# A list of its own for the second and third hop of a graph propagation, and the first hop's sums moved out in pieces

## The chip, the cores and the metric
One core of one Trainium2 chip runs the program once. The metric is the device time of that execution in microseconds (us). The engines are TensorE (PE, with its weight loads PEld), VectorE (DVE), ScalarE (ACT), GpSimd (POOL) and SyncE (SP, which here only issues DMAs). DVE-, ACT-, POOL- or PEq in the profile is an engine's sequencer.

## The reference
A graph has 100,000 nodes with 32 features (`x`) and 25,000 edges `src -> dst`, sorted by `dst`. Four layers follow each other, each with a layer norm behind it: a tensor-product convolution with a small radial network, a three-hop propagation, an edge network with a maximum per node, and an attention layer. The change is in the second:

```
deg = segment_sum(ones, dst);  norm = deg[src]**-.5 * deg[dst]**-.5   (0 where deg is 0)
x = weight;  acc = weight
for _ in range(3):
    x = segment_sum(norm[:, None] * x[src], dst)
    acc = acc + x
return acc / 4
```

Only nodes that some edge points to have a value after the first hop, so an edge carries something in the second hop only if its source has an incoming edge, in the third only if that edge's source has one too.

## The kernel before
**Layout.** Edges lie in tiles of 128 partitions by T = 196 columns, in order of `dst`; the sums of a run of equal `dst` are scans along the columns, one VectorE instruction for each of 32 features (L1378), with a "seam" (L1331) that carries a run over from one partition to the next through two small TensorE transposes. Values are fetched by row with indirect DMAs, one column of 128 rows per instruction, issued by POOL. Nodes that no edge points to need no edges; their layers collapse to a chain of norms and products, done in "node chunks" (13 of 128 x 60 rows and a tail of 40 x 4 rows): TensorE turns and multiplies (L1136), ScalarE copies and squares (L867), VectorE reduces and scales (L1731). `node_chunks` (L426) runs them; `NODE_PAIRS` (L423) says which pairs of chunks run in which of four windows: two pairs, two pairs, two pairs, and the last chunk with the tail.

**Start.** VectorE zeroes A_dst, SP stores it as zeros to `edge_sums` and tables 1 and 2 (L472), 3,136 KB each, then loads the 20 weights (L489); VectorE waits for those (L1463) before it folds them and starts the histogram of `dst`. POOL waits for the zeros (L658) before it gathers into A_dst.

**Short list.** `make_short` (L1557, VectorE, within the first layer) picks in each partition the edges whose source has an incoming edge, and moves them to the front in order with MAX8 and MATCH_REPLACE (`take_top`, L1606) on three keys: the table index, the flags and degree, and the output column. The longest partition gives n. FEWEST = 60 columns are always moved, FEW = 64 are computed; if n is larger, branches handle up to T columns.

**Propagation.** `short_columns` (L676, POOL) moves the list's columns and then raises `short_in`. Per hop k = 0, 1, 2 (L699) POOL waits for the table and for a free buffer, then gathers 60 columns. VectorE does its node window, waits for `short_in`, and runs `propagate` (L1767): scan, clear the buffer for the next gather, seam, multiplication by dinv_short, add to A_tmp, multiplication again for the table, which SP stores (L546 to L552). After the third hop POOL scatters the accumulated sums A_tmp to `edge_sums`, again 60 columns (L707). SP loads `edge_sums` back into A_msg by seven chunks, then the edge attributes into A_tmp (L554 to L560). VectorE meanwhile computes statistics of A_src (L1797 to L1812), then `add_layer1` (L1813) adds the sums to A_dst, `norm` normalises chunk by chunk, and SP stores each chunk to table 3 (L561). POOL's 196 gathers of the next layer wait for that table (L712); it then sends a quad of four columns at a time and waits for the quad before the last to land.

ScalarE and TensorE follow the same windows in order (L885, L1162); a seam stands behind each.

Of the kernel before, what the change touches and what calls it, by code (L numbers as in the profile page):

```python
# [31 lines left out]
FEWEST = 60  # L32
TOP = -(-T // 8) * 8
# [22 lines left out]
def parts_until(k):  # L56
    return sum(TABLE_PARTS[:k + 1])
# [19 lines left out]
def gnn_kernel(nc, x, src, dst, r_feat, rel, edge_attr, edge_weight, w1, b1, w2, b2,  # L77
# [12 lines left out]
    with ExitStack() as ctx:  # L90
# [13 lines left out]
        tables = [dram(f"table_{k}", (E_PAD, FEAT if k else FEAT + 1)) for k in range(5)]  # L104
# [66 lines left out]
        n_short = sb("n_short", [1, 1], i32)  # L171
        row_base = sb("row_base", [P, 1])
# [7 lines left out]
        diag = sb("diag", [P, P])  # L180
        seam_state = sb("seam_state", [32, P])
# [49 lines left out]
        few_done, more_done, rest_done = sem("few_done"), sem("more_done"), sem("rest_done")  # L231
        short_in = sem("short_in")
# [55 lines left out]
        short_row_i = dst_f[:].bitcast(i32)  # L288

# [133 lines left out]
        NODE_PAIRS = [(0, 2, False), (2, 4, False), (4, 6, False), (6, D_CHUNKS // 2, True)]  # L423
# [30 lines left out]
        def _(sp):  # L454
# [17 lines left out]
            for zeroed in (edge_sums, tables[1], tables[2]):  # L472
                sp.dma_start(zeroed.rearrange(main3, t=T), A_dst[:]).then_inc(zeros_stored, 16)
# [72 lines left out]
            for k in (1, 2):  # L546
                sp.wait_ge(table_ready, parts_until(k))
                table = tables[k].rearrange(main3, t=T)
                with sp.If(n > FEW):
                    sp.dma_start(table, A_sum[:]).then_inc(table_stored, 16)  # L550
                with sp.Else():
                    sp.dma_start(table[:, 0:FEW, :], A_sum[:, 0:FEW, :]).then_inc(table_stored, 16)  # L552
                node_chunks(sp, load_nodes, ahead[k], ahead[k + 1], k == 2)
# [35 lines left out]
        def _(pool):  # L589
# [68 lines left out]
            pool.wait_ge(zeros_stored, 48)  # L658
# [15 lines left out]
            turns = [0]  # L674

            def short_columns(move, keep=None):  # L676
                turns[0] += 1
                for t in range(FEWEST):
                    if keep and keep(t):
                        pool.wait_ge(n_out, keep(t))  # L680
                    move(t).then_inc(few_done, 16)
                with pool.If(n > FEWEST):
                    for t in range(FEWEST, FEW):
                        move(t).then_inc(more_done, 16)
                    pool.wait_ge(more_done, 16 * (FEW - FEWEST) * turns[0])
                with pool.If(n > FEW):
                    for t in range(FEW, T):
                        move(t).then_inc(rest_done, 16)
                    pool.wait_ge(rest_done, 16 * (T - FEW) * turns[0])
                pool.wait_ge(few_done, 16 * FEWEST * turns[0])  # L690
# [8 lines left out]
            for k in range(3):  # L699

                pool.wait_ge(table_stored, 16 * parts_until(k))
                pool.wait_ge(gather_ok, k + 2)
                to, idx = (A_msg, idx_next) if k else (msg_wide, idx_short)
                short_columns(take_short(lambda t: to[:, t, :], tables[k], idx),
                              None if k else lambda t: max(t - 24, 0) // 15)
            pool.wait_ge(acc_ready, 1)
            short_columns(lambda t: pool.indirect_dma_start(  # L707
                out=edge_sums, out_offset=bass.IndirectOffsetOnAxis(ap=out_short[:, t:t + 1], axis=0),
                in_=A_tmp[:, t, :], in_offset=None, bounds_check=edge_limit, oob_is_err=False))
# [29 lines left out]
        def _(act):  # L739
# [144 lines left out]

            for window in NODE_PAIRS:  # L885
                nodes(*window)
# [146 lines left out]
        def _(pe):  # L1033
# [229 lines left out]
        def _(v):  # L1263
# [293 lines left out]
            def make_short():  # L1557
# [76 lines left out]
                step(ts(dinv_short[:], keys[:, 0, :].bitcast(i32), 1.0, ALU.max))  # L1634

# [5 lines left out]
                step(ts(keys[:, 0, :].bitcast(i32), top_i[:, 2, own], 255, ALU.bitwise_and))  # L1641
                step(ts(run, keys[:, 0, :].bitcast(i32), row_base[:], ALU.add, float(-SKIP), ALU.add))
# [124 lines left out]
            def propagate(k, width):  # L1767

                a_sum, a_msg, acc = A_sum[:, 0:width, :], A_msg[:, 0:width, :], A_tmp[:, 0:width, :]
                by = bcast(dinv_short[:, 0:width], FEAT)  # L1770
                if k == 0:
                    v.tensor_copy(idx_next[:, 0:width], msg_wide[:, 0:width, FEAT].bitcast(i32))
                step(scan(a_sum, a_msg if k else msg_wide[:, 0:width, 0:FEAT], same_short, ALU.mult, ALU.add, 0.0))
                if k < 2:
                    v.memset(a_msg, 0.0).then_inc(gather_ok, 1)
                seam(a_sum, FEAT, 0, 1, in_first_short, ALU.mult, ALU.add, 0.0)
                step(tt(a_sum, a_sum, by, ALU.mult))
                ins = tt(acc, acc, a_sum, ALU.add) if k else v.tensor_copy(acc, a_sum)
                if k < 2:
                    step(ins)  # L1780
                    done(tt(a_sum, a_sum, by, ALU.mult), table_ready, parts_until(k + 1))
                else:
# [327 lines left out]
```

## Time and profile before

| what | us |
|---|---|
| median of 3 runs | 2012.31 (2007.58 to 2029.45) |
| profiled execution | 2009.45 |
| its span, first to last instruction | 2007.7 |
| POOL busy | 1419.7 |
| VectorE busy | 1323.3 |
| TensorE busy | 1026.2 |

Idle time of an engine is shown in brackets with what ended it. "Chain" is the sequence of work that ended last, followed back from the end. An indirect DMA's time on POOL is the making of its descriptors, not the transfer; the chain shows a transfer as DMA from issue to landing. "issue" is time in which an engine waited for nothing that the profile shows.

### The profile page before, as it was taken

To read this page: it belongs to the slowest core of one execution; us is meant where nothing else is said; L and a number is where in the kernel's file an instruction comes from. 1 tells how busy PE (TensorE), PEld (TensorE's weight loads), DVE (VectorE), ACT (ScalarE), POOL (GpSimd) and SP (SyncE) were. 2 spreads that over 40 slices of the span, in tenths; PEclk is the share of its full clock that TensorE was granted. 3 is DMA by queue.
4 is the path that set the end of the run, shared out by engine and by line. 5 is a ranking of instruction groups with operands and counts; after the bars stand their busy time and mean duration, and the time that the engine had idled before them with its cause. 6 is when DMAs were issued, how large, how long until landed. Compare 5 with 4: busy or idle time off the path is not lost.

```text
span 2007.7 us, 15353 instructions
## 1 busy us (share of the span) xinstructions
PE 1026.2 (51%) x3969; PEld 700.3 (35%) x3969; DVE 1323.3 (66%) x3061; ACT 468.6 (23%) x989; POOL 1419.7 (71%) x1304
## 2 busy tenths in 40 slices
PE   0989737872770353407020069888458767613100
PEld 0334414441430353406020035545257767613000
DVE  6989949998999774727364653435667788875000
ACT  0954301110110341405121122222112233311000
POOL 7887777775778484855757277777277777777776
PEclk9985555555555676859565555555555555655555
DMA  7008611110002231303100600000001110100000
GB/s 261 11 11 286 216 12 13 13 13 9 12 13 67 89 112 64 119 21 121 42 27 8 193 4 4 22 13 13 29 22 27 27 24 25 27 11 11 11 11 10
DMA packets 65924, 101.54 MB, mean 51 GB/s; under 512 B 35491, under 2 KB 54693, under 8 KB 65060
## 3 DMA queue, kind: packets, MB, share of 16 engines
q1 hardware_dynamic: 23074, 74.87, 10.7%
q0 software_dynamic: 40832, 12.83, 4.6%
q10 hardware_dynamic: 1922, 12.80, 1.6%
q8 instruction: 31, 0.51, 0.1%
q14 instruction: 65, 0.53, 0.1%
HBM read 55.72 MB, written 52.06 MB: 54 GB/s over the span
## 4 chain that ended last, share of the span: by engine, by line
POOL 41%; DVE 30%; issue 16%; PE 8%; DMA 3%; SPq 2%; ACT 0%; POOLq 0%; DVEq 0%; PEld 0%; PEldq 0%; ACTq 0%
POOL A_src L626 17%; POOL A_msg L694 11%; POOL out L733 10%; DVE work L1279 9%; DVE work L1290 6%; PE bank L1078 4%; POOL edge_sums L707 4%; DVE A_sum L1378 2%; DVE A_dst L1279 2%; DVE stat L1290 1%; DVE A_msg L1279 1%; SPq L489 1%; PE bank L1035 1%; DVE A_tmp L1279 1%; DVE A_sum L1279 1%
## 5 line engine op out<-in xcount | busy, mean ns | idle before, releaser
L626 POOL DMA_INDIRECT A_src<-table,pos_i x392 | 424.4, 1083 | 193.1 <-issue 122.8
L626 POOL DMA_INDIRECT A_dst<-in_x,dst_i x196 | 225.3, 1149 | 75.4 <-issue 58.3
L1118 PE MATMUL bank<-w2fold,work 65*128 65x384 f32 x392 | 262.2, 849 | 3.6 <-ACT work L811 3.1
L1035 PE MATMUL bank<-ident,work 128*65 128x128 f32 (+2 forms) x592 | 153.0, 390 | 197.0 <-DVE work L1279 106.4
L733 POOL DMA_INDIRECT out<-A_dst,out_i x196 | 201.5, 1028 | 62.4 <-issue 62.4
L1290 DVE TENSOR_REDUCE work<-work 128x96 f32<-128x768 f32 (+5 forms) x245 | 210.4, 907 | 49.6 <-ACT work L840 41.4
L694 POOL DMA_INDIRECT A_msg<-table,idx_next x120 | 147.7, 1231 | 89.0 <-DMA table<-A_sum 50.4
L1035 PE MATMUL bank<-ident,end_col 128*32 128x128 f32 (+2 forms) x16 | 6.0, 377 | 397.0 <-DVE end_col L1335 392.9
L1035 PEld LDWEIGHTS bank<-ident,work 128*65 128x65 f32 (+2 forms) x592 | 98.5, 194 | 260.2 <-DVE work L1279 142.1
L626 POOL DMA_INDIRECT A_src<-x_pos,A_tmp x140 | 145.2, 1037 | 46.6 <-issue 46.3
L1279 DVE TENSOR_TENSOR work<-bank,work 128x256 f32<-128x256 f32 (+1 forms) x392 | 164.0, 477 | 4.6 <-PE bank L1118 4.6
L1118 PEld LDWEIGHTS bank<-w2fold,work 65*128 65x128 f32 x392 | 124.0, 331 | 96.8 <-issue 89.8
L1157 PE MATMUL bank<-nodes_w,small 128*128 128x128 f32 (+1 forms) x784 | 119.6, 313 | 45.2 <-ACT small L830 45.0
L1035 PEld LDWEIGHTS bank<-ident,end_col 128*32 128x32 f32 (+2 forms) x16 | 1.5, 92 | 400.1 <-DVE end_col L1335 395.5
L1287 DVE SCALAR_TENSOR_TENSOR A_sum<-A_sum,same_pen,bank 128x32 f32<-128x32 f32 x195 | 48.2, 247 | 134.0 <-PE bank L1191 128.8
L811 ACT ACTIVATE work<-bank,b1col 65x256 f32<-65x256 f32 x98 | 45.9, 470 | 378.2 <-PE bank L1035 378.0
L1157 PEld LDWEIGHTS bank<-nodes_w,small 128*128 128x128 f32 (+1 forms) x784 | 110.5, 224 | 53.6 <-ACT small L830 53.6
L1191 PEld LDWEIGHTS bank<-mw,work 65*128 65x128 f32 x392 | 87.3, 328 | 77.2 <-issue 77.2
L694 POOL DMA_INDIRECT A_msg<-table,nxt_i x60 | 73.6, 1227 | 42.3 <-DMA table<-A_tmp 24.3
L707 POOL DMA_INDIRECT edge_sums<-A_tmp,out_short x60 | 73.4, 1223 | 37.3 <-issue 20.6
L1184 PE MATMUL bank<-work,mw 96*64 96x512 f32 x98 | 96.5, 1087 | 0.0
L1191 PE MATMUL bank<-mw,work 65*128 65x32 f32 x392 | 93.7, 404 | 0.0
(298 smaller groups left out, 2231.5 us busy)
## 6 DMA issues: line engine op xcount, KB each, us to landing
work<-in_x SPq DMA_DIRECT2D x26, 960.0 KB
x_pos<-A_sum SPq DMA_DIRECT2D x13, 990.0 KB, 5.3
out<-work ACTq DMA_DIRECT2D x13, 960.0 KB, 3.8
table<-A_dst SPq DMA_DIRECT2D x2, 3136.0 KB, 22.7
table<-A_dst SPq DMA_DIRECT2D x14, 448.0 KB, 4.0
A_src<-table,pos_i POOLq DMA_INDIRECT x392, 2.3
A_tmp<-in_edge_attr_2x SPq DMA_DIRECT2D x49, 112.0 KB
table<-A_tmp SPq DMA_DIRECT2D x7, 462.0 KB, 2.5
```

Source lines behind the costliest of these rows:

```text
L626: pool.indirect_dma_start(out=column(t), out_offset=None, in_=of, in_offset=bass.IndirectOffsetOnAxis(ap=idx[:, t:t + 1], axis=0), bounds_ ...
L694: return lambda t: pool.indirect_dma_start(out=column(t), out_offset=None, in_=of, in_offset=bass.IndirectOffsetOnAxis(ap=idx[:, t:t + 1], ...
L707: short_columns(lambda t: pool.indirect_dma_start(out=edge_sums, out_offset=bass.IndirectOffsetOnAxis(ap=out_short[:, t:t + 1], axis=0), i ...
L733: pool.indirect_dma_start(out=out, out_offset=bass.IndirectOffsetOnAxis(ap=out_i[:, t:t + 1], axis=0), in_=A_dst[:, t, :], in_offset=None, ...
L1035: return nc.tensor.transpose(out_ap, in_ap, ident[0:n, 0:n])
L1078: last = nc.tensor.matmul(banks[6 + h][:, 0:half], lo_hot[:, 2 * slot + j, :], hi_hot[:, 2 * slot + j, h * half:(h + 1) * half], start=Fal ...
L1118: last = nc.tensor.matmul(banks[2 + 2 * slot + j][:, 0:PATHS], hidT[:, slot, j * P:(j + 1) * P], w2fold[:], start=True, stop=True)
L1157: last = nc.tensor.matmul(banks[2 + 2 * w + s][0:parts, k * P:(k + 1) * P], n_xT[:, s, k * parts:(k + 1) * parts], nodes_w[:, w * P:(w + 1 ...
L1184: nc.tensor.matmul(banks[2 + slot][0:HID0, :], mw1[:], catT[:, slot, :], start=True, stop=True).then_inc(e_h, 1)
L1191: last = nc.tensor.matmul(banks[4 + slot][:, j * FEAT:(j + 1) * FEAT], hidT2[:, slot, j * P:(j + 1) * P], mw2[:], start=True, stop=True)
L1279: return v.tensor_tensor(out=o, in0=a, in1=b, op=op)
L1290: return v.tensor_reduce(out=o, in_=a, axis=AX, op=op)
```

## The change
A second list is built in VectorE after the first hop: of the short list's edges those whose source's own sum has a source in the list, at most FEWEST2 = 22 columns moved and FEW2 = 24 computed. The first hop fetches with each value the row's place in the short list; table 1 gets a 33rd column with the place in the second list. The first hop's sums no longer join the accumulator: they are scattered from A_sum to `edge_sums`, 12 columns after the first hop, 12 behind the second hop's gathers, 36 behind the third's. The second and third hop's sums go to a buffer `edge_sums2`, 22 columns. Both are loaded back and added one after the other. `edge_sums2` and the wider table 1 must be zeroed too. Node windows become three pairs, one, one, and the rest (chunks 10 to 12 and tail). The edge attributes are loaded after the exchange of table 3. If a partition's second list is longer than 24, `use_short_list` goes on with all T columns.

```diff
+FEW2 = 24
+FEWEST2 = 22
+FIRST_OUT = [12, 24]
...
-        NODE_PAIRS = [(0, 2, False), (2, 4, False), (4, 6, False), (6, D_CHUNKS // 2, True)]
+        NODE_PAIRS = [(0, 3, False), (3, 4, False), (4, 5, False), (5, D_CHUNKS // 2, True)]
...
-            for zeroed in (edge_sums, tables[1], tables[2]):
+            wide = tables[1].rearrange("(p t) f -> p (t f)", t=T)
+            sp.dma_start(wide[:, 0:T * FEAT], flat(A_dst[:])).then_inc(zeros_stored, 16)
+            sp.dma_start(wide[:, T * FEAT:], A_dst[:, 0:T // FEAT + 1, :].rearrange("p t f -> p (t f)")[:, 0:T]).then_inc(zeros_stored, 16)
+            for zeroed in (edge_sums, edge_sums2, tables[2]):
...
+            sp.wait_ge(first_hop_out, 16 * FEWEST)
             sp.wait_ge(short_in, 4)
+            sp.wait_ge(acc_ready, 1)
             for c in range(CHUNKS):
                 sp.dma_start(chunk(A_msg, c), chunk(edge_sums.rearrange(main3, t=T), c)).then_inc(sums_in[c], 16)
+            sp.wait_ge(hop_done, 16 * FEWEST2 * 3)
+            sp.wait_ge(short_in, 5)
+            for c in range(CHUNKS):
+                sp.dma_start(chunk(A_tmp, c), chunk(edge_sums2.rearrange(main3, t=T), c)).then_inc(sums2_in[c], 16)
+            exchange(3, A_dst)
             for a, b in PIECES:
                 sp.dma_start(A_tmp[a:b], edge_attr[a * T:b * T, :].rearrange(main3, t=T)).then_inc(ea_in, 16)
...
-            exchange(3, A_dst)
             exchange(4, A_dst, LAST_ORDER)
...
+            first_out = put_short(edge_sums, out_short, lambda t: A_sum[:, t, :])
+            pool.wait_ge(first_hop_ready, 1)
+            short_columns(first_out, first_hop_out, range(FIRST_OUT[0]))
+            pool.wait_ge(table_stored, 16 * parts_until(1))
+            pool.wait_ge(gather_ok, 3)
+            n2 = pool.value_load(n_short2[0:1, 0:1], min_val=0, max_val=T)
+            second_columns(take_short(lambda t: msg_wide[:, t, :], tables[1], idx2))
+            short_columns(first_out, first_hop_out, range(*FIRST_OUT))
+            pool.wait_ge(table_stored, 16 * parts_until(2))
+            pool.wait_ge(gather_ok, 4)
+            second_columns(take_short(lambda t: A_msg[:, t, :], tables[2], idx2))
+            short_columns(first_out, first_hop_out, range(FIRST_OUT[1], FEWEST))
             pool.wait_ge(acc_ready, 1)
+            second_columns(put_short(edge_sums2, out2, lambda t: A_tmp[:, t, :]))
...
+            nodes(*NODE_PAIRS[0])
+            next_root(1.0)
+            for window in NODE_PAIRS[1:]:
                 nodes(*window)
...
+                if first == 0:
+                    pe.wait_ge(count_ready, 2)
+                    turn(banks[6][0:1, 0:P], end_col[:, 0:1], P).then_inc(count_turned, 1)
...
+            def first_hop(width):
+
+                a_sum, by = A_sum[:, 0:width, :], bcast(dinv_short[:, 0:width], FEAT)
+                v.tensor_copy(idx_next[:], msg_wide[:, :, FEAT].bitcast(i32))
+                step(scan(a_sum, msg_wide[:, 0:width, 0:FEAT], same_short, ALU.mult, ALU.add, 0.0))
                 seam(a_sum, FEAT, 0, 1, in_first_short, ALU.mult, ALU.add, 0.0)
+                done(tt(a_sum, a_sum, by, ALU.mult), first_hop_ready, 1)
+                tt(tmp_wide[:, 0:width, 0:FEAT], a_sum, by, ALU.mult)
+
+            def second_list():
+
+                step(v.tensor_copy(idx_f, idx_next[:, 0:FEW]))
+                step(ts(kept2, idx_f, SKIP / 2, ALU.is_lt))
+                step(tt(kept2, kept2, ends_row, ALU.max))
+                step(v.memset(kept2[:, 0:1], 1.0))
+                done(total(end_col[:, 0:1], kept2), count_ready, 2)
...
+                for r in range(FEW2 // 8):
+                    at = slice(8 * r, 8 * r + 8)
+                    for k in range(3):
+                        ins = v.max(out=top2[:, k, at], in_=keys2[:, k, :])
                     step(ins)
+                    for k in range(3):
+                        ins = v.match_replace(out=keys2[:, k, :], in_to_replace=top2[:, k, at], in_values=keys2[:, k, :],
+                                              imm_value=0.0)
+                    step(ins)
...
+            def use_second_list():
+
+                few = slice(0, FEW2)
+                v.tensor_copy(dinv2[:, few], std[:, few])
+                v.tensor_copy(idx2[:, few], idx2_new)
+                step(v.memset(msg_wide[:, few, :], 0.0))
+                v.memset(msg_wide[:, few, FEAT].bitcast(i32), SKIP).then_inc(gather_ok, 1)
+                done(v.tensor_copy(stat[:, few], dinv2[:, few]), table_ready, parts_until(1))
+
+            def second_hop(width, to_table):
+
+                acc, by = A_tmp[:, 0:width, :], bcast(dinv2[:, 0:width], FEAT)
+                v.tensor_copy(idx2[:, 0:width], msg_wide[:, 0:width, FEAT].bitcast(i32))
+                step(scan(acc, msg_wide[:, 0:width, 0:FEAT], same2, ALU.mult, ALU.add, 0.0))
+                if width == FEW2:
+                    v.memset(A_msg[:, 0:width, :], 0.0).then_inc(gather_ok, 1)
+                seam(acc, FEAT, 0, 1, in_first2, ALU.mult, ALU.add, 0.0)
+                step(tt(acc, acc, by, ALU.mult))
+                done(tt(to_table, acc, by, ALU.mult), table_ready, parts_until(2))
...
+            v.wait_ge(count_turned, 2)
+            step(total(end_col[0:1, 1:2], banks[6][0:1, 0:P], ALU.max))
+            root(v.tensor_copy(n_short2[:], end_col[0:1, 1:2]))
+            n2 = v.value_load(n_short2[0:1, 0:1], min_val=0, max_val=T)
...
             node_chunks(v, nodes, *NODE_PAIRS[3])
 
+
+            for c in range(CHUNKS):
+                v.wait_ge(sums_in[c], 16)
+                last = stt(chunk(A_dst, c), chunk(A_msg, c), 0.25, chunk(A_dst, c), ALU.mult, ALU.add)
+            step(last)
...
             def add_layer1(c):
-                v.wait_ge(sums_in[c], 16)
-                return stt(chunk(A_dst, c), chunk(A_msg, c), 0.25, chunk(A_dst, c), ALU.mult, ALU.add)
+                v.wait_ge(sums2_in[c], 16)
+                return stt(chunk(A_dst, c), chunk(A_tmp, c), 0.25, chunk(A_dst, c), ALU.mult, ALU.add)
```

`make_short` gets six more small operations that keep, for 64 columns, what the second list needs. The third hop does what the second does without the memset and the table, and adds its sums to the second's.

## Rows read from the trace of the kernel before

**Rows 1.** The page of the profile: busy times, and chain by line
```profile
PE 1026.2 (51%) x3969; PEld 700.3 (35%) x3969; DVE 1323.3 (66%) x3061; ACT 468.6 (23%) x989; POOL 1419.7 (71%) x1304
...
POOL A_src L626 17%; POOL A_msg L694 11%; POOL out L733 10%; DVE work L1279 9%; DVE work L1290 6%; PE bank L1078 4%; POOL edge_sums L707 4%; DVE A_sum L1378 2%; DVE A_dst L1279 2%; DVE stat L1290 1%; DVE A_msg L1279 1%; SPq L489 1%; PE bank L1035 1%; DVE A_tmp L1279 1%; DVE A_sum L1279 1%
```

**Rows 2.** The page's costliest groups: moves of a list's columns
```profile
L694 POOL DMA_INDIRECT A_msg<-table,idx_next x120 | 147.7, 1231 | 89.0 <-DMA table<-A_sum 50.4
...
L707 POOL DMA_INDIRECT edge_sums<-A_tmp,out_short x60 | 73.4, 1223 | 37.3 <-issue 20.6
```

**Rows 3.** DVE's timeline, 694 to 797 us: start, duration, instruction, idle before
```profile
694.22 2.15 DVE L1290 TENSOR_REDUCE work<-work 128x60 f32<-128x1920 f32 x1 [10.88 <-ACT work L840]
...
743.56 2.15 DVE L1290 TENSOR_REDUCE work<-work 128x60 f32<-128x1920 f32 x1 [1.38 <-ACT work L840]
...
754.44 2.16 DVE L1279 TENSOR_TENSOR work<-work 128x1920 f32<-128x1920 f32 x1
773.57 0.22 DVE L1772 COPY idx_next<-A_msg 128x64 int32<-128x64 int32 x1 [16.98 <-POOLq L691]
...
780.15 1.76 DVE L1775 MEMSET A_msg<- 128x2048 f32 x1 [0.49 <-DVE A_sum L1378]
...
785.38 2.29 DVE L1279 TENSOR_TENSOR A_sum<-A_sum,small 128x2048 f32<-128x2048 f32 x1 [0.24 <-DVE A_sum L1279]
...
796.59 2.15 DVE L1290 TENSOR_REDUCE work<-work 128x60 f32<-128x1920 f32 x1 [5.33 <-ACT work L840]
```

**Rows 4.** POOL's timeline, 796 to 883 us, same columns
```profile
796.47 0.99 POOL L694 DMA_INDIRECT A_msg<-table,idx_next  x1 [24.68 <-DMA table<-A_sum]
797.76 1.00 POOL L694 DMA_INDIRECT A_msg<-table,idx_next  x1 [0.30 <-issue]
...
882.41 1.00 POOL L694 DMA_INDIRECT A_msg<-table,idx_next  x1 [2.95 <-issue]
```

**Rows 5.** Window of one move: length, busy PE, PEld, DVE, ACT, POOL, clock, DMA share, GB/s
```profile
796.00:892.50 96.50, 30.12 (x219) 27.89 (x219) 48.13 (x36) 28.39 (x62) 74.12 (x60) 0.71 0.23 81
```

**Rows 6.** The chain in order of time, 770 to 1124 us: start, duration, what
```profile
770.79 2.12 DMA A_msg<-table,nxt_i
...
791.45 4.75 DMA table<-A_sum
...
1120.32 3.42 DMA A_msg<-edge_sums
```

**Rows 7.** DVE's timeline, 1047 to 1124 us
```profile
1047.38 6.68 DVE L1290 TENSOR_REDUCE stat<-A_src 128x196 f32<-128x6272 f32 x1
...
1054.39 6.71 DVE L1279 TENSOR_TENSOR A_src<-A_src,stat 128x6272 f32<-128x6272 f32 x1
...
1078.02 6.69 DVE L1279 TENSOR_TENSOR A_src<-A_src,small 128x6272 f32<-128x6272 f32 x1
1123.84 2.11 DVE L1287 SCALAR_TENSOR_TENSOR A_dst<-A_msg,A_dst 128x896 f32<-128x896 f32 x2 [39.12 <-DMA A_msg<-edge_sums]
```

**Rows 8.** DVE's timeline in the making of the first list, 479 to 490 us
```profile
479.31 0.89 DVE L1609 MAX8 A_sum<-A_sum 128x8 f32<-128x196 f32 x3
...
486.44 0.47 DVE L1623 CAST A_sum<-A_sum 128x600 int32<-128x600 f32 x1 [3.06 <-DVEq L1622]
...
489.54 0.26 DVE L1283 TENSOR_SCALAR small<-A_sum 128x196 f32<-128x196 int32 x1
```

**Rows 9.** POOL's timeline beside a long DVE multiplication, and the gather's start
```profile
1055.67 6.29 POOL L707 DMA_INDIRECT edge_sums<-A_tmp,out_short  x1 [0.31 <-issue]
...
1152.87 2.31 POOL L626 DMA_INDIRECT A_src<-table,pos_i  x1 [33.73 <-DMA table<-A_dst]
```

**Rows 10.** SP's timeline, the stores of zeros
```profile
8.52 0.90 SPq L473 DMA_DIRECT2D table<-A_dst  x2
```

**Rows 11.** The chain in order of time, before the histogram
```profile
34.40 6.80 DMA gw<-in_L_gnn_W
```

**Rows 12.** Window in the stores of zeros, columns as in rows 5
```profile
20.00:25.00 5.00, 0.70 (x3) 0.26 (x2) 2.11 (x8) 0.00 (x0) 3.78 (x5) 1.00 1.07 430
```

More of the change, by code:

```diff
@@ L171, in gnn_kernel @@
         n_short = sb("n_short", [1, 1], i32)
+        n_short2 = sb("n_short2", [1, 1], i32)
+        end_column, edges_in, ends_row = (r3[:, FEW * k:FEW * (k + 1)] for k in range(3))
+        same2, in_first2, dinv2, idx2, out2 = dst_f, r3, dinv, idx_next, nxt_i
         row_base = sb("row_base", [P, 1])
@@ L180, in gnn_kernel @@
         diag = sb("diag", [P, P])
+        slot_key, slot_ones = diag[:, 0:FEW], diag[:, FEW:2 * FEW]
         seam_state = sb("seam_state", [32, P])
@@ L673, in _, with short_columns @@
             n = pool.value_load(n_short[0:1, 0:1], min_val=0, max_val=T)
[L674 to L678, printed above, removed]
+            turns = {"short": 0, "second": 0}
+            def short_columns(move, done, columns, keep=None):
+                for t in columns:
                     if keep and keep(t):
                         pool.wait_ge(n_out, keep(t))
-                    move(t).then_inc(few_done, 16)
+                    move(t).then_inc(done, 16)
+                if columns.stop < FEWEST:
+                    return
+                turns["short"] += 1
                 with pool.If(n > FEWEST):
@@ L688, in short_columns, with second_columns @@
                         move(t).then_inc(rest_done, 16)
-                    pool.wait_ge(rest_done, 16 * (T - FEW) * turns[0])
-                pool.wait_ge(few_done, 16 * FEWEST * turns[0])
+                    pool.wait_ge(rest_done, 16 * (T - FEW) * turns["short"])
+                pool.sem_inc(short_in, 1)
+            def second_columns(move):
+                turns["second"] += 1
+                for t in range(FEWEST2):
+                    move(t).then_inc(hop_done, 16)
+                with pool.If(n2 > FEWEST2):
+                    for t in range(FEWEST2, FEW2):
+                        move(t).then_inc(hop_more, 16)
+                    pool.wait_ge(hop_more, 16 * (FEW2 - FEWEST2) * turns["second"])
+                with pool.If(n2 > FEW2):
+                    for t in range(FEW2, T):
+                        move(t).then_inc(hop_rest, 16)
+                    pool.wait_ge(hop_rest, 16 * (T - FEW2) * turns["second"])
                 pool.sem_inc(short_in, 1)
@@ new lines, in third_hop @@
+            def third_hop(width):
+                acc, msg, by = A_tmp[:, 0:width, :], A_msg[:, 0:width, :], bcast(dinv2[:, 0:width], FEAT)
+                step(scan(msg, msg, same2, ALU.mult, ALU.add, 0.0))
+                seam(msg, FEAT, 0, 1, in_first2, ALU.mult, ALU.add, 0.0)
+                step(tt(msg, msg, by, ALU.mult))
+                done(tt(acc, acc, msg, ALU.add), acc_ready, 1)
+            node_chunks(v, nodes, *NODE_PAIRS[0])
+            v.wait_ge(few_done, 16 * FEWEST)
+            v.wait_ge(short_in, 1)
@@ new lines, in _ @@
+            before_it = dict(count)
+            seq_after = count["seq"] + 100
+            with v.If(n > FEW):
+                first_hop(T)
+                step(v.memset(stat[:], 1.0))
+                done(v.memset(end_col[:, 0:1], float(T)), count_ready, 2)
+                v.sem_inc(dve_seq, seq_after - count["seq"])
+            count.update(before_it)
+            with v.Else():
+                first_hop(FEW)
+                second_list()
+                v.sem_inc(dve_seq, seq_after - count["seq"])
@@ L1786, in _ @@
+            with v.If(n2 > FEW2):
+                use_short_list()
+                v.sem_inc(dve_seq, seq_after - count["seq"])
+            count.update(before_it)
+            with v.Else():
+                use_second_list()
+                v.sem_inc(dve_seq, seq_after - count["seq"])
+            count["seq"] = seq_after
+            for k, hop in ((1, lambda width: second_hop(width, A_msg[:] if width == T else A_msg[:, FEW:FEW + FEW2, :])),
+                           (2, third_hop)):
                 node_chunks(v, nodes, *NODE_PAIRS[k])
+                v.wait_ge(hop_done, 16 * FEWEST2 * k)
```

136 lines of the change are left out of this document (97 added, 39 removed).

## The prediction

> **What bounds the kernel now.** I read the page first [rows 1]: POOL is the busiest engine (71%) and carries the chain of work that ended last; the lines this change touches, L694 and L707, hold 11% and 4% of it. In the costliest groups [rows 2] these are four moves of 60 columns, at 1.23 us of descriptor work per column. Then the timeline: in the first node window VectorE handles a chunk every (743.56 - 694.22) / 3 = 16.4 us, is done at 754.44 + 2.16 = 756.6 and idles 16.98 us until POOL's last column has landed [rows 3]. A bare column costs 1.00 + 0.30 = 1.30 us, 60 cost 78 us [rows 4], yet the move fills a window of 96.5 us: it has one gap of 2.95 us [rows 4], a landing, and columns that are stretched while VectorE multiplies, 74.1 us of busy time instead of 60 [rows 5], or 3.5 us for each of the four node chunks. After a move come the hop's sums on VectorE and a store of 4.75 us; only then does POOL start again [rows 3, 4, 6], 24.68 us after it stopped. After the last move VectorE has been idle for 39.12 us [rows 7]. So from 680 to 1124 us POOL's columns and the gaps between hops set the time, and VectorE's work hides beside them. What the change is worth is read there: at 1124 us everything behind follows as before.
>
> **Part by part.** All on the clock of the profiled execution, shifts of the start left for later.
>
> *First window, one chunk pair longer.* Two chunks more: 756.6 + 2 x 16.4 = 789.4. The first hop, which started at 773.57, now waits for VectorE: 16 us lost.
>
> *First hop.* From the copy of the next indices to the first multiplication it took 785.38 - 773.57 = 11.8 us, of which the memset and its wait (2.0) go; with the multiplication (2.3) the sums are ready at 789.4 + 9.8 + 2.3 = 801.5 [rows 3]. POOL then issues 12 scatters (12 x 1.30 = 15.6, about 2 more beside the second multiplication) and is done at 819, before it is needed.
>
> *Second list.* New on the path: a multiplication (2.3); some 39 small operations and 3 rounds of MAX8 and replacing, at 64 or 24 columns; count, turn and a root with a reciprocal over 196 columns; register loads, two branches; a memset of 24 columns. At 196 columns a small operation takes 0.26 us and three MAX8 0.89, and leaving a branch cost 3.06 us [rows 8]. Upper bound: 39 x 0.3 + 3 x 2.05 + 4 + 3 x 3.1 + 4 = 35 us; lower, at 0.15 us each and branches for nothing: 17 us. I take 24: the operations are a third as wide but have a fixed part, and the branch behind the seam cost 0.24 us [rows 3]. Table ready at 825.5, stored (wider rows, same count, 4.75 plus issue [rows 6]) at 830.7; POOL loads its register and gathers from 831.7. ScalarE's root stands ahead of the next window, so that window's first chunk is ready only some 12 us after 820 (before, it came 796.59 - 785.38 = 11.2 us after the seam [rows 3]).
>
> *Hop 2.* 22 columns x 1.30 = 28.6, plus 6 for one and a half node chunks beside it: landed at 867.4. VectorE's two chunks end at 833 + 16.4 + 13 = 862, in time (a last chunk takes 756.6 - 743.56 = 13). The sums: 11.8 us with a smaller memset, 10.7, and two multiplications of 24 columns at 0.9: 12.4, so 880.5. Its scans stay 32 instructions, and I claim nothing for their being narrower. The store of 384 KB takes about 3 us. POOL meanwhile issues 12 scatters: two skipped branches (3, by the gap of rows 4), 15.6 and 1.4 of stretching: 886.3. Here POOL is last by 3 us.
>
> *Hop 3.* 28.6 + 7.2: landed 923.4; VectorE's two chunks, ready 11.2 us after the seam at 879, end at 920. Sums without memset: 0.7 to start, 9.8 + 1.8, so 935.7, with the seam done at 933.9.
>
> *Last window.* Chunks 10 to 12 and the tail (the old last window was one chunk and tail): first reduction at 933.9 + 11.2 = 945.1, end 945.1 + 2 x 16.4 + 13 + 3 = 994 (3 is what I put for the tail of 40 partitions and 4 rows). POOL's 36 scatters run beside it: 923.4 + 3 + 46.8 + 9 = 982, landed and loaded back (3.42 [rows 6]) at 988, so hidden. VectorE then adds seven chunks (7 x 1.09) and does the statistics of A_src, which ran from 1047.38 to 1078.02 + 6.69 = 1084.7, 37.3 us [rows 7], hidden beside POOL before and exposed now: 994 + 7.6 + 37.3 = 1039.
>
> *Last scatter.* 22 columns from 982: 28.6 plus stretching by VectorE's two-input operations. One such operation on all of A_src (6.71 us) held one column for 6.29 us [rows 7, 9]. With 14 us of stretching, landing and load: about 1031. Hidden by 8 us.
>
> The norm began at 1123.84 [rows 7], now at 1039: **84.8 us gained**. The Trainium skill (SBUF — State Buffer, Who interferes with whom) infers that a two-input tensor operation does not stall descriptor generation; rows 7 and 9 show that it does here, and the row decides: I give the page's rule no chance of its own. By the page hop 2 and hop 3 would each lose their stretching, and the sum would be some 10 us lower.
>
> *Zeros.* SP issues two more large stores ahead of the weight loads, 3.3 MB more. Issue alone is 0.45 us each [rows 10], 0.9. VectorE waits for the last weight at 41.2 us, on the chain [rows 11]. The stores run at 430 GB/s with all DMA engines full [rows 12], so 3.3 MB are 7.7 us if the weights queue wholly behind them. I take 4, since the last weight's 6.80 us already hold some queueing, and keep 0.9 and 8. The Trainium skill (DMA: Bandwidth & Descriptors, Queues, rings and completion order) says that descriptors of one ring are consumed in order; that speaks for the upper end, and would put the sum 4 us higher.
>
> *First list.* Six more small operations on VectorE, on the chain: 6 x 0.2 = 1 us (0 to 2).
>
> *Edge attributes.* Their load, 3.1 MB, moves behind the exchange of table 3. The exchange loses that company (it took 1152.87 - 1123.84 = 29 us to the first gather [rows 7, 9]; 0 to 3 us gained), while the load, 7.5 to 12 us by 430 GB/s or a load's lower rate, meets the first gathers of the next stage. I take +0.5 in all, bounds -3 and +10. VectorE needs the attributes 25 us later, after the spread.
>
> Sum: -84.8 + 4 + 1 + 0.5 = -79.3. The profiled execution took 2009.45 us (span 2007.7), so 1930; the median shown is 2.9 above it: **1933 us**.
>
> **Rivals.**
> *POOL stays last.* For: its last scatter has 8 us of slack in a sum with 40 us of stretching and skipped branches, and the gap of 2.95 us may come at every one of six branches. Against: the VectorE side is a sum of measured pieces. If POOL needs 20 us more, 12 show: 1945.
> *The edge attributes collide.* POOL waits for quads to land, and the next stage goes at POOL's pace. If nothing lands for the load's 12 us: 1933 + 10 = 1943. Against: with the DMA engines full of zeros POOL issued gathers at its usual pace, 3.78 us busy in 5 [rows 12], though nothing made it wait for them to land.
> *The weights wait for all the zeros.* The stores fill the engines [rows 12] and the weights come behind them on the same queue: 7.7 us instead of 4, 1937. Against: the last weight landed some 8 us after the stores' time was up (9.6 MB by 430 GB/s from 8.5 us), so it does not simply come behind them. This is what the page's rule of ring order gives.
> *The zeros cost nothing and the list is cheap (17 us).* 1933 - 3 - 7 = 1923.
> *The other side: the second list does not fit.* If one partition keeps over 24 columns, both hops and the second scatter move 196 columns. Then 60 + 3 x 196 columns stand where 180 stood: 468 x 1.30 = 608 us more, 2620 us. It decides at 25. The trace cannot show it; counting the reference's edges by the rule of the diff gives at most 22 kept columns, 12.7 on average, so nearly excluded. It is also the way in which the change would not do what it says.
>
> **How the numbers follow.** Forecast case 0.50; weights wait for all zeros 0.10; POOL last 0.15; collision 0.10; cheap list and zeros 0.08; not fitting 0.01; the rest, 0.06, for a wait that I have not seen. The range goes from 1916 (all lower bounds: list -7, zeros -3, edge attributes -3, narrower scans -4) to 1958 (list +11 and a rival's 12). A measurement here tells about 1% from no change. Faster by over 1% needs under 1992, which all cases but the last two give: 0.95. Within 1%: 0.03. Slower: 0.02.
>
> **What would show it.** Right: POOL's gathers of the two hops at 22 columns in some 35 us each; first sums ready at 801.5 instead of 787.7, plus the start's shift; in hop 3's wake VectorE busy without a gap up to the norm; the norm at about 1039 plus 5. Wrong: VectorE idle before the norm (POOL still last); more than 30 us between the first hop's sums and its table; the histogram starting over 8 us later; POOL's gaps between the first quads. Gathers of 196 columns would break the forecast altogether.

## The result and the profile after

The changed kernel took 1928.20 us (median of 4 runs, 1922.72 to 1943.07) against 2009.94 us for the kernel before on the same chip: ratio 0.959, 95% interval 0.950 to 0.967. The profiled execution took 1925.58 us, its span is 1923.8 us. Forecast were 1933 us, 1930 on the profile's own clock. Later, on another chip, the ratio was 0.959 again (0.955 to 0.962), and on one more 1.013; that one has a place of its own below.

The page, busy times and two of the costliest groups, as in [rows 1, 2]:

```profile
PE 1020.9 (53%) x3970; PEld 696.9 (36%) x3970; DVE 1330.1 (69%) x3146; ACT 466.6 (24%) x990; POOL 1366.5 (71%) x1250
...
L747 POOL DMA_INDIRECT edge_sums<-A_sum,out_short x60 | 74.0, 1234 | 51.0 <-DVE A_sum L1345 33.0
...
L741 POOL DMA_INDIRECT A_msg<-table,nxt_i x60 | 73.4, 1224 | 40.0 <-DMA table<-A_tmp 22.1
```

A column costs what it did. POOL lost 53 us of busy time, 54 columns; that the time fell by 84 says that gaps went too. Where the end of the stage now comes from, DVE's timeline shows; its last row answers to the last of [rows 7]:

```profile
799.52 0.34 DVE L1842 COPY idx_next<-A_msg 128x196 int32<-128x196 int32 x1 [0.83 <-DVE work L1345]
...
841.13 2.15 DVE L1356 TENSOR_REDUCE work<-work 128x60 f32<-128x1920 f32 x1 [9.25 <-ACT work L901]
...
874.84 0.41 DVE L1929 COPY idx_next<-A_msg 128x24 int32<-128x24 int32 x1 [4.40 <-DMA A_msg<-table,idx_next]
...
928.72 3.66 DVE L1444 TENSOR_TENSOR_SCAN A_msg<-dst_f,A_msg 128x24 f32<-128x24 f32 x32 [6.49 <-DMA A_msg<-table,idx_next]
...
1003.76 6.69 DVE L1356 TENSOR_REDUCE stat<-A_src 128x196 f32<-128x6272 f32 x1
...
1010.77 6.69 DVE L1345 TENSOR_TENSOR A_src<-A_src,stat 128x6272 f32<-128x6272 f32 x1
...
1034.39 6.69 DVE L1345 TENSOR_TENSOR A_src<-A_src,small 128x6272 f32<-128x6272 f32 x1
1041.12 2.09 DVE L1353 SCALAR_TENSOR_TENSOR A_dst<-A_tmp,A_dst 128x896 f32<-128x896 f32 x2
```

The norm's first row has no bracket: before, VectorE had stood still for 39.12 us there [rows 7], now it comes straight from the statistics. It is VectorE that sets this end; its only waits for POOL's data behind the first window are 4.40 and 6.49 us, in front of the second and third hop. Its other long waits there are of 9 us each, when a window's first chunk comes through TensorE and ScalarE, and one of 5.57 us for ScalarE's squares within the statistics. Inside hops 2 and 3 POOL's gathers still land last, by those 4.40 and 6.49 us; from the third hop's sums on, VectorE has no wait for POOL's data.

The time splits into three parts, by three rows that both kernels have: POOL's first column of the first hop (680.16 before, 687.82 now), the norm (1123.84 and 1041.12), the end.

| stretch | predicted | measured |
|---|---|---|
| start to POOL's first column | +5 | +7.7 |
| from there to the norm | -84.8 | -90.4 |
| from the norm to the end | +0.5 | -1.2 |
| sum | -79.3 | -83.9 |

How far such a split can be trusted, a second profile of the changed kernel shows, on the chip of run 12:

```profile
1037.63 2.09 DVE L1353 SCALAR_TENSOR_TENSOR A_dst<-A_tmp,A_dst 128x896 f32<-128x896 f32 x2
```

Its first column came at 686.95 us, the norm 3.5 us earlier than here, and from the norm to the end it took 891.5 us, not 882.7. So 3 or 4 us at the norm, and more behind it, lie within what one kernel shows from one profile and chip to the next.

The start, DVE's timeline and then SP's in the stores of zeros:

```profile
49.68 0.82 DVE L1349 TENSOR_SCALAR w2fold<-A_tmp 65x64 f32<-65x64 f32 x6 [8.95 <-DMA gw<-in_L_gnn_W]
```

```profile
31.47 8.14 SPq L508 DMA_DIRECT2D gb<-in_L_gnn_b  x1
39.65 3.81 SPq L508 DMA_DIRECT2D gw<-in_L_gnn_W  x4
```

VectorE is ready at 40.7 us and waits 8.95 us for the last four weights, which SP came to only at 39.65 us: the issue before them took 8.14 us instead of the 1.1 to 1.3 of its neighbours.

### The profile page after: what moved, and what is told of

Its sections match the earlier page's. It is cut to its first block, busy times and chain, and to the rows that moved or that the text cites. A ratio compares the mean times of both kernels' runs of the same rounds, so it can differ in the third digit from the quotient of the medians.

```text
span 1923.8 us, 15361 instructions
## 1 busy us (share of the span) xinstructions
PE 1020.9 (53%) x3970; PEld 696.9 (36%) x3970; DVE 1330.1 (69%) x3146; ACT 466.6 (24%) x990; POOL 1366.5 (71%) x1250
## 4 chain that ended last, share of the span: by engine, by line
POOL 28%; issue 10%; DVE 9%; PE 5%; DMA 3%; ACT 1%; POOLq 0%; DVEq 0%; ACTq 0%; SPq 0%
POOL A_src L656 15%; POOL out L794 10%; POOL A_msg L741 3%; DMA A_src<-table,pos_i 2%; DVE work L1345 2%; PE bank L1257 1%; PE bank L1250 1%; DVE stat L1356 1%; PE bank L1098 1%; DVE A_dst L1345 1%; DVE A_dst L1353 1%; DVE A_src L1345 1%; PE bank L1220 1%; DVE A_sum L2156 1%; POOL edge_sums L747 0%
## 5 line engine op out<-in xcount | busy, mean ns | idle before, releaser
L656 POOL DMA_INDIRECT A_dst<-in_x,dst_i x196 | 230.3, 1175 | 76.2 <-issue 58.5
L1098 PEld LDWEIGHTS bank<-ident,work 128*65 128x65 f32 (+2 forms) x592 | 95.7, 190 | 267.5 <-DVE work L1345 142.8
L747 POOL DMA_INDIRECT edge_sums<-A_sum,out_short x60 | 74.0, 1234 | 51.0 <-DVE A_sum L1345 33.0
L1098 PE MATMUL bank<-ident,A_tmp 128*65 128x128 f32 (+1 forms) x203 | 50.4, 398 | 72.6 <-DVE A_tmp L2104 66.4
```

Of the source, the lines that this page charges most:

```text
L656: pool.indirect_dma_start(out=column(t), out_offset=None, in_=of, in_offset=bass.IndirectOffsetOnAxis(ap=idx[:, t:t + 1], axis=0), bounds_ ...
L747: return lambda t: pool.indirect_dma_start(out=of, out_offset=bass.IndirectOffsetOnAxis(ap=idx[:, t:t + 1], axis=0), in_=column(t), in_off ...
L1098: return nc.tensor.transpose(out_ap, in_ap, ident[0:n, 0:n])
```

## Experiments

All edits are to the changed kernel. Times of single profiled runs are named as such. The runs were made on several chips: the kernel before took 2003.11 us (7 runs) where runs 1 to 4 were made and 2009.00 us (7 runs) at runs 5 to 7, so times across them are compared as ratios to it.

**1. The weights ahead of all zeros.** SP's block of stores moves behind the loop of weight loads:

```diff
-            for zeroed in (edge_sums, edge_sums2, tables[2]): ...
             for to, of in (... weights ...):
                 sp.dma_start(to, of).then_inc(loaded_w, 16)
+            for zeroed in (edge_sums, edge_sums2, tables[2]): ...
```

> SP loads the 20 weights ahead of the five stores of zeros. Theory (the weights stood behind the zeros in SP's queue, and nothing else was late at the start): VectorE's wait of 8.95 us at 49.68 us goes wholly, so it folds the weights from about 40.7 us and the rest follows; time 1925.6 - 9 = 1917 us. The zeros land some 3 us later, which nobody sees, since POOL first needs them much later. Rival (the DMA engines' load as a whole delays the start, or something else is as late): the fold starts no earlier than about 45 us, 1921 to 1926 us.

Measured: VectorE folds the weights at 40.76 us with no wait, 8.9 us earlier. The norm starts at 1029.51 us, 11.6 us earlier, and the profiled run took 1912.68 us, 12.9 less than the changed kernel's, some of which may be the chip's. By median 1918.51 us, ratio 0.958 (0.953 to 0.964), which by itself tells nothing from 0.959: in times the gain is not resolved, in the trace the wait is gone and what follows is earlier. Of the 2.7 us that came on top by the norm, 1.7 are the first window's six chunks, which took 95.7 us instead of 97.4; run 12's profile of the changed kernel has 95.5, so this need not be the edit's.

**2. Only one store behind the weights.**

```diff
-            for zeroed in (edge_sums, edge_sums2, tables[2]):
+            for zeroed in (edge_sums, tables[2]):
...
+            sp.dma_start(edge_sums2.rearrange(main3, t=T), A_dst[:]).then_inc(zeros_stored, 16)
```

> Only the store of zeros to edge_sums2 (3.2 MB) goes behind the weights; the wider zeros of table 1 stay ahead. Theory (the delay is the time of the bytes ahead of the weights, 3.2 MB by some 415 GB/s = 7.7 us): VectorE's wait falls from 8.95 to between 0.6 and 1.5 us, time 1918 us. Rival (the wider table with its extra small store, or SP's waits for a free place in the queue, make the delay): over 3 us of the wait stay.

Measured, 1913.65 us in one run:

```profile
41.27 0.73 DVE L1350 TENSOR_SCALAR w2fold<-A_tmp 65x64 f32<-65x64 f32 x6 [0.55 <-DMA gw<-in_L_gnn_W]
```

The wait falls by 8.4 us with this one store of 3.2 MB, and the issue that took 8.14 us takes 1.33. The wider table 1 and its small extra store cost nothing that shows, so one more DMA ahead is not what delays. The delay fits the time of the bytes queued ahead: 3.2 MB at the 414 GB/s that moved between 10 and 40 us would be an estimated 7.7 us.

**3. The node windows of before.** `NODE_PAIRS` is two, two, two pairs, and the rest.

> The node windows of the kernel before (two, two, two pairs, the rest) with everything else of the change. Theory (VectorE's work with its gaps sets the time from the first hop to the norm, POOL is hidden): the first hop comes some 16 us earlier (VectorE idle that long in the first window), in exchange VectorE's waits of 4.4 and 6.5 us for POOL go, net 16 - 11 = 5 us more: norm at 1046, time 1931 us. Rival (POOL's columns set it, as before the change): the first hop's 16 us come through whole, 1910 us.

Measured: 1934.81 us, ratio 0.965 (0.959 to 0.972), norm at 1049.41. First window and second hop:

```profile
783.66 0.34 DVE L1842 COPY idx_next<-A_msg 128x196 int32<-128x196 int32 x1 [19.49 <-DMA A_msg<-table,nxt_i]
...
888.52 0.18 DVE L1929 COPY idx_next<-A_msg 128x24 int32<-128x24 int32 x1 [0.50 <-DVE work L1345]
```

The first hop comes 15.9 us earlier and the norm 8.3 later. The two waits for POOL are gone, as expected. The rival falls: POOL's columns no longer set this stretch. The 8.3 us are more than the 5 reckoned because the first window's wait is 19.49 us and not 16. Against 0.83 there that is 18.7 us more, while 3.9 and 5.7 us go in front of the second and third hop: 9.1 net. By the profiles the new windows are worth 8 us (12 by run 12's); the intervals of the medians overlap.

**4. A pair more in the third window**, (0, 3), (3, 4), (4, 6), the rest.

> Windows of three, one, two pairs, and the rest: the third window takes a pair from the last. Theory (VectorE bound): its wait of 6.49 us for the third hop's columns is filled with node work, the norm starts 6.5 us earlier, 1919 us; POOL's last scatter can start only at about 971 us instead of 938, but POOL has 36 others to send until 983 us. Rival (POOL or its landing decides the end): no gain or a loss, 1926 us or more.

Measured: 1925.81 us, ratio 0.960 (0.955 to 0.965); norm at 1037.66, 3.5 us earlier, 0.9 of them already there by the second hop. But run 12's profile of the changed kernel has it at 1037.63 too, so no gain is shown and the theory's 6.5 us did not come: the rival "no gain" stands. The node work does end 6.6 us earlier (3.1 against run 12), but then a new wait stands in VectorE's queue:

```profile
994.94 1.09 DVE L1353 SCALAR_TENSOR_TENSOR A_dst<-A_msg,A_dst 128x896 f32<-128x896 f32 x1 [1.79 <-DMA A_msg<-edge_sums]
996.82 2.20 DVE L1353 SCALAR_TENSOR_TENSOR A_dst<-A_msg,A_dst 128x896 f32<-128x896 f32 x2 [0.78 <-DMA A_msg<-edge_sums]
999.18 1.09 DVE L1353 SCALAR_TENSOR_TENSOR A_dst<-A_msg,A_dst 128x896 f32<-128x896 f32 x1 [0.17 <-DMA A_msg<-edge_sums]
```

These are the adds of the first hop's sums. The last of the 36 scatters behind the third hop's gathers stands at 982.60 us, and SP issues the load back at 984.73. The last chunk landed only at 999.16. In the changed kernel SP issued at 984.41 and the adds began at 996.62, so these scatters had an estimated 4 us of cover, less than the last scatter has, because the adds stand ahead of the statistics.

**5. No pieces:** `FIRST_OUT = [0, 0]`.

> All 60 scatters of the first hop's sums behind the third hop's gathers (FIRST_OUT 0 and 0), the rest as changed. Theory (the pieces fill time in which POOL has nothing else to do): 24 more columns stand in POOL's tail, 24 x 1.3 to 1.6 us = 31 to 38 us, less 3 us because the third hop's gathers start by the table's store. The last scatter ends about 1052 to 1059 us instead of 1023.5, landed and loaded back it holds VectorE until 1057 to 1064: norm 16 to 23 us later, time 1941 to 1949 us. Rival (VectorE hides the tail whole): 1926 us.

Measured, 1943.44 us in one run, norm at 1063.27, 22 us later, at the upper end:

```profile
1017.82 2.16 DVE L1353 SCALAR_TENSOR_TENSOR A_dst<-A_msg,A_dst 128x896 f32<-128x896 f32 x2 [25.69 <-DMA A_msg<-edge_sums]
```

The size was right, the place not. VectorE waits for the first hop's sums, and the norm, behind it, has no wait for the second scatter. So the pieces are worth 22 us, since all 37 us of statistics queue behind the adds.

**6. The second list as long as the first:** `FEW2 = 64`, `FEWEST2 = 60`.

> The second list is made as before but with 64 columns computed and 60 moved, so that the second and third hop and their scatter move as many columns as in the kernel before, while the first hop's sums still leave on their own. Theory (the gain is the 38 columns fewer per move, and the separate first scatter alone costs): five more rounds of MAX8 (12 us), two gathers longer by 38 columns (about 54 us each with their stretching), a tail of 36 and 60 scatters (some 150 us behind the third hop's landing, less the 30 us that VectorE hides now): norm about 170 us later, time 2090 us, range 2070 to 2110, slower than the kernel before. Rival (the separate scatter and the windows carry a part of the gain): under 2009 us.

Measured: 2082.60 us in one run, slower than the kernel before. The second hop, the third, and the norm:

```profile
933.07 0.22 DVE L1929 COPY idx_next<-A_msg 128x64 int32<-128x64 int32 x1 [58.49 <-DMA A_msg<-table,idx_next]
...
1041.22 6.04 DVE L1444 TENSOR_TENSOR_SCAN A_msg<-dst_f,A_msg 128x64 f32<-128x64 f32 x32 [57.15 <-DMA A_msg<-table,idx_next]
...
1198.46 2.13 DVE L1353 SCALAR_TENSOR_TENSOR A_dst<-A_tmp,A_dst 128x896 f32<-128x896 f32 x2 [44.29 <-DMA A_tmp<-edge_sums]
```

Without shorter moves the rest of the change costs 74 us (2082.60 against 2009.00 for the kernel before on that chip; the longer list's own rounds are in it): POOL's second scatter alone is exposed by 44 us. The whole gain, and more, is the 38 columns fewer in three moves.

**7. The statistics of A_src early**, windows two, two, two, the rest; the result for `r3` is kept in a spare 196 words of the work buffer:

```diff
+            step(total(stat[:], A_src[:]))
             node_chunks(v, nodes, *NODE_PAIRS[0])
+            ... centre, square, roots (what stood before add_layer1) ...
             v.wait_ge(few_done, 16 * FEWEST)
...
+                if k == 1:
+                    tt(A_src[:], A_src[:], bcast(r1, FEAT), ALU.mult)
                 node_chunks(v, nodes, *NODE_PAIRS[k])
```

> The statistics of A_src (37.3 us of VectorE, in front of the norm in the changed kernel) move: first reduction in the gap before the first node chunk, centring, squares and roots behind the first window, the last multiplication in the gap before the second; windows two, two, two, and the rest, so that they fall into VectorE's idle time of some 19 us there. Theory (VectorE bounds the way to the norm): first hop at about 786 us, third hop's sums at about 968, node chunks done at 994, the norm at 1001 to 1008 us instead of 1041, time 1888 us, 1882 to 1895. Rival (POOL's columns come right behind VectorE): the last scatter, now started at 968 us, and its way back hold the norm until 1015 us or later, 1900 us or more.

Measured: 1921.65 us, ratio 0.957 (0.952 to 0.961).

```profile
1011.41 7.11 DVE L1354 SCALAR_TENSOR_TENSOR A_dst<-A_msg,A_dst 128x896 f32<-128x896 f32 x7
...
1036.91 2.12 DVE L1354 SCALAR_TENSOR_TENSOR A_dst<-A_tmp,A_dst 128x896 f32<-128x896 f32 x2 [18.09 <-DMA A_tmp<-edge_sums]
```

The rival was right. VectorE is done at 1018.5 us and waits for POOL, whose last scatter began behind the third hop's sums. My 994 us for the node chunks had also left out the 12.5 us of the first hop's own sums: they ended at 1011. With VectorE relieved, POOL bounds again. By these intervals the run is not told from the changed kernel.

**8 to 10. On another chip.** The changed kernel again, then run 7 with windows two, two, one, the rest and `FIRST_OUT = [12, 40]`, then this with the weights first.

> The changed kernel itself once more, on the chip of the two that follow, as their measure: 1925 us, norm at about 1041 us on the profile's clock.

> The run with early statistics showed that VectorE ended at 1018.5 us but waited 18.09 us for POOL's last scatter, which could not start before the third hop's sums, behind two pairs of node chunks. Here the third window has one pair again (two, two, one, the rest), and the second piece of the first hop's scatters has 28 columns, not 12 (FIRST_OUT 12 and 40), in a window in which POOL idled 26.84 us. Theory (VectorE's sum plus POOL's tail behind the third hop): third hop's sums some 33 us earlier, about 952 us; POOL sends 20 and 22 columns from 943 to about 1000, loaded back by 1005; VectorE adds the first sums at 1011 to 1018.5 without a wait, norm at 1019 us, time 1904 us. Rival (the window now waits for POOL's gathers as the changed kernel's did, 4 to 6 us, and more two-input work beside POOL stretches its columns): norm at 1026 us or later, 1911 us or more.

> The run before it together with the weights ahead of the zeros. Theory (the two are independent): the norm another 9 to 11.6 us earlier, as with the weights first alone: 1008 to 1010 us, time 1893 to 1895 us. Rival (what the start gives is lost behind a fixed point, POOL's first gathers): 1900 us or more.

Measured: 2446.15, 2404.47 and 2396.47 us, while the kernel before took 2418.26 there (21 runs, 2402.88 to 2434.56): ratios 1.013 (1.009 to 1.017), 0.994 (0.991 to 0.997) and 0.993 (0.989 to 0.996). The times forecast can't be read here. Still, runs 9 and 10 beat the changed kernel on the same chip, intervals apart; between the two of them nothing is resolved. The changed kernel's page, and its third and fourth window on DVE's timeline:

```profile
PE 1081.8 (44%) x3970; PEld 737.3 (30%) x3970; DVE 1332.4 (55%) x3146; ACT 470.2 (19%) x990; POOL 1311.7 (54%) x1250
...
DVE 34%; another core or an unknown queue 25%; PE 18%; issue 16%; ACT 3%; POOL 2%; DMA 1%; DVEq 0%; ACTq 0%; SPq 0%; POOLq 0%
```

```profile
1222.13 2.15 DVE L1356 TENSOR_REDUCE work<-work 128x60 f32<-128x1920 f32 x1 [64.70 <-issue]
...
1248.06 0.53 DVE L1815 RECIPROCAL work<-work 128x60 f32<-128x60 f32 x1 [23.77 <-ACT work L912]
...
1314.81 2.15 DVE L1356 TENSOR_REDUCE work<-work 128x60 f32<-128x1920 f32 x1 [30.87 <-ACT work L901]
```

VectorE is busy for 1332 us as ever; the 520 us by which the span is longer are gaps. The first window's six chunks take 97.9 us from the first reduction to the hop's copy, and 97.4 on the first chip. But the reductions that open the first, third and fourth window come 50.97, 64.70 and 30.87 us after the instruction before them, where the first chip had 9 to 11; the second window's comes after 8.53 as ever. The six chunks in a row lose nothing, but in the third window 23.77 us more go between two instructions of a chunk. So the stalls come few and long, many of them where engines go on to other code, though not at every such place. The rows put them down to ScalarE or to nothing that the profile knows ("issue"), the chain 41% to "issue" and "another core or an unknown queue". What slows the chip is not shown, nor why the change loses 1% there; the kernel before was only timed on it, not profiled.

**11 and 12. Everything, and the changed kernel, on a chip of the first kind.**

> The kernel with everything (early statistics, windows two, two, one, the rest, pieces 12 and 40, weights first) once more, since on the chip of the three runs before every kernel took a fifth longer and engines waited where they entered new code. Theory (on a chip that behaves as in the profiles first read, VectorE's sum sets the norm): norm at 1008 to 1010 us, time 1893 to 1895 us, 0.942 of the kernel before. Rival (POOL's gathers and stretched columns gate it): norm at 1015 us or later, 1900 us or more. If the chip is again of the slow kind: about 0.9925 of the kernel before, as measured there.

> The changed kernel on the same chip as the run before it: 0.9586 of the kernel before, some 1925 us, if the chip behaves as in the profiles first read; 1.013 if it is of the slow kind.

Measured: 1902.66 us (1900.07 to 1921.57), ratio 0.947 (0.943 to 0.951), against 1931.23 us and 0.959 (0.955 to 0.962) for the changed kernel and 2011.97 for the one before. So a version beats both: 28.6 us by the medians under the changed kernel, intervals apart. It missed its forecast and came out in the rival's range, though VectorE and not POOL is the last at the norm:

```profile
936.93 3.66 DVE L1445 TENSOR_TENSOR_SCAN A_msg<-dst_f,A_msg 128x24 f32<-128x24 f32 x32 [7.79 <-DMA A_msg<-table,idx_next]
...
979.88 0.53 DVE L1816 RECIPROCAL work<-work 128x60 f32<-128x60 f32 x1 [6.34 <-ACT work L913]
...
1017.66 2.09 DVE L1354 SCALAR_TENSOR_TENSOR A_dst<-A_tmp,A_dst 128x896 f32<-128x896 f32 x2
```

The norm starts at 1017.66 us instead of 1009 with VectorE the last again; 7.79 us of that are the wait for POOL in the third window. There POOL came from 28 scatters straight into the gathers, at 899.13 us, 5.4 us after the table had landed. But with 12 scatters the changed kernel is 4.1 us late at that place and waits 6.49, so the longer piece explains little of it. Another 6.34 us went in the last window, behind ScalarE, which had itself waited for a store of node output. Beside run 1 (norm at 1029.51) the moved 37 us brought 12: from POOL's first column to the norm VectorE is busy as before, 241.8 us against 241.4, and its idle time fell from 109.6 us to 97.6. What is left lies in many waits, the longest 9.51 us, and not in one gap that the statistics could fill.

## Why the prediction was right

The time was 5 us under the forecast and well inside the range, with the mechanism as predicted: POOL's columns shrink, gaps between hops shrink with them, and the end of the stage goes over to VectorE's node work, adds and 37.3 us of statistics. Within hops 2 and 3 POOL's gathers stay last, as the sum had it (by 5.4 and 3.4 us; measured 4.40 and 6.49). Run 6 shows that the shorter moves carry the gain. That VectorE sets the end is shown by the norm's row without a wait and by run 3, where idle time added in the first window comes back at the norm. Run 7 shows how near POOL is behind: with the statistics moved away, the norm came 4 us earlier and waited for POOL. By its steps:

- **First window, longer by a pair.** 789.4 was put for its end, 109.2 us behind POOL's first column; it was 110.9 (798.7 - 687.8), since its chunks went at 16.7 us, not 16.4. The sums were ready 124.2 us behind it, not 121.3.
- **Second list, 24 us.** It took 19.9 (811.97 to 831.89). The small operations were over-rated: mostly 0.18 to 0.25 us each, a round of MAX8 and replacing 1.2, and no branch cost the 3.06 of [rows 8]; the longest gap is 0.89.
- **Hop 2 and hop 3.** From POOL's first column to VectorE's release the gathers took 37.2 us each (35.7 and 37.1 forecast). The sums were two to three us cheaper than the 12.4 (10.1 and 9.3): I had claimed nothing for the scans' width, but 32 scans of 24 columns took 3.65 us, against 5.95 for 64.
- **Skipped branches, 3 us.** Wrong, they cost nothing: the second hop's last gather, twelve scatters and the third hop's gather follow each other in steps of 0.30. The gap of 2.95 in [rows 4] was no branch's price either: it stands between two gathers of one move. POOL was last by 4 us all the same.
- **Last window, adds and statistics.** 58.6 us from the third hop's sums to the tail's end (predicted 58.3), then 44.5 to the norm (44.9). Right within half a microsecond.
- **Last scatter.** Its last column ended at 1023.5, in run 7 the way back took 4.7 us more; so about 1028, 13 us hidden and not 8.
- **Zeros, 4 us.** Mis-sized: 8.4 at the fold; by POOL's first column 7.7 with the first list's small operations, for which 1 us more had been put. The rival "the weights wait for all the zeros", to which I gave 0.10, was right, and run 2 settles it. My evidence against it was that the last weight landed 8 us after the stores' time was up (by the figures given it is 10: 8.5 + 22.3 = 30.8, against 41.2). But by [rows 11] that weight was issued only at 34.40 us, so its landing said nothing of how long it would stand behind more bytes. The Trainium skill (DMA: Bandwidth & Descriptors, Queues, rings and completion order) has descriptors of one ring consumed in order; runs 1 and 2 agree.
- **Edge attributes, +0.5.** From the norm to the first gather 27.5 us, not 29; then the first column took 3.87 us, not 2.31, and another 4.48. The tenth gather stands 3.7 us further behind the norm than before, the last of the 196 only 0.8. So the load does lie beside the first gathers (mean DMA share 0.95 to 1.03 in each 5 us from 1064 to 1079 us), but what they lose is made up for, and the collision rival's 10 us fall. The -1.2 by the end is less than the difference between two profiles of the changed kernel. The load was not moved by itself: the buffer it goes to is in use until the adds are done.
- **Range.** Its upper end does not follow from its terms: 1933 + 11 + 12 is 1956, not 1958. Nothing hangs on it.

Two errors, +2.7 at the start and -5.6 in the propagation, went against each other, and within the propagation +2.8 in the first window went against -4 in the list and -5 in the sums. That the total came within 5 us is in part luck.

**Two-input operations beside POOL.** The forecast let rows 7 and 9 decide against the Trainium skill (SBUF — State Buffer, Who interferes with whom). The trace after shows it more cleanly, since three kinds of work on tiles of one size follow each other beside POOL:

```profile
1002.88 1.70 POOL L747 DMA_INDIRECT edge_sums<-A_tmp,nxt_i  x1 [0.30 <-issue]
1004.88 0.98 POOL L747 DMA_INDIRECT edge_sums<-A_tmp,nxt_i  x1 [0.30 <-issue]
...
1011.32 7.01 POOL L747 DMA_INDIRECT edge_sums<-A_tmp,nxt_i  x1 [0.30 <-issue]
1018.63 0.98 POOL L747 DMA_INDIRECT edge_sums<-A_tmp,nxt_i  x1 [0.30 <-issue]
```

Beside the reduction (1003.76 to 1010.45, one input) columns take 0.98 us; beside the TENSOR_TENSOR (1010.77, two inputs) one column takes 7.01, as long as the operation; beside ScalarE's squares, which follow until 1023, 0.98 again. The page infers that such an operation leaves descriptor work alone. Here the column is held for as long as the operation runs.

## What to carry to other kernels

When one engine's chain is cut, add up the next one's with its gaps, and ask in which order its queue stands: the statistics behind the adds made the first hop's scatters, not the last scatter, the nearest edge (runs 4 and 5). A large store that nobody waits for yet can delay the loads issued behind it on its queue, here by 8.4 us for 3.2 MB (run 2), so put loads that start the work first. Work hidden beside a bound engine comes out when that engine gets faster; moving it forward earns only the idle time that it fills, 12 us of 37 here, and can hand the bound back (run 7). And profile the same kernel twice before reading a few microseconds: run 4's 3.5 us at the norm also lie between two profiles of one kernel.

## What was not expected of the hardware

- An issue of a small load on SP took 8.14 us behind 13 MB of stores, and the load after it was the one that VectorE waited for.
- Branches that are skipped on POOL left no gap beyond the usual 0.30 us, where 3 us had been put.
- One chip took 1.20 times as long for the same kernel before (2418 against 2010 us), with the loss in gaps: in the changed kernel's profiles VectorE and ScalarE are busy within 1% as long on both, TensorE 6% longer, POOL 4% less. A gain of 4% on two chips was a loss of 1% there.
